# First layer of a graph network kernel: the messages and a copy of the run flags in two free PSUM banks

## The chip, the cores and the metric

The kernel runs on one core of a Trainium2 chip. The metric is the device time of one execution in microseconds, the median of several runs. The core has five engines that run their own instruction streams and meet on semaphores: TensorE (PE: matmuls, and PEld: its weight loads), VectorE (DVE), ScalarE (ACT), GpSimd (POOL) and SyncE (SP, which here issues plain DMAs). POOL also issues the indirect DMAs, those that take their addresses from a table of indices in SBUF. PSUM has eight banks; a bank holds 512 fp32 elements in each of 128 partitions.

## The reference, cut to what matters

Four graph layers on 12500 nodes with 16 features and 400000 edges, each preceded by a layer norm and a ReLU. The change touches the first layer only, which applies the weighted adjacency four times:

```python
def step(y, _):
    msg = weights[:, None] * y[col]
    y_new = jax.ops.segment_sum(msg, row, num_segments=N_NODES)
    return (y_new, None)
y, _ = jax.lax.scan(step, x, None, length=LAYER_NUMBER)   # LAYER_NUMBER = 4
```

Here `col` is the edge's `dst`, by which the edges come sorted, and `row` its `src`.

## The kernel before, in words

The function `powers` computes the first layer in four rounds, one for each application. Before it the edges have been put into an order by their target: 132 turns (`G_TURNS`), each of 25 columns of 128 edges (`TURN`). Two turns make a pair (`PAIR`), 66 pairs a round, 264 pairs in all. Within a partition the edges of a turn lie so that those that read the same node follow each other as a run. So a node's row has to be written only where a run starts; a scan along the columns carries it through the run. `goes_on` holds the run flags (0 where a run starts, 1 where it goes on; a 16-bit type).

In each round the engines do this:

- POOL scatters the node rows from SBUF (`by_b`) to the places in HBM (`filled`) at which runs start, with one indirect DMA for 128 rows (line 1651), addresses from the table `at_start` in SBUF. The rows are cut into blocks of 8 such DMAs (2 in the last block of each of the 7 groups of 13 blocks), 91 blocks and 686 DMAs a round. After every 6 DMAs it rests (ten tiny memsets and a wait). It also gathers the first row of each turn (`first`, line 1654), 132 DMAs a round. When all DMAs of a block have landed, it raises `blocks_ready` (line 1631), and it does so behind the issues of the block after it.
- SP waits, turn by turn, for `blocks_ready` to reach the block that the turn needs, and for `expanded`, by which VectorE tells that one of four buffers is free (lines 1606 and 1607), and loads the turn's 25 columns into `given`.
- VectorE takes a pair at a time: it waits for the pair's two loads, puts the first rows in (line 1676), runs 16 scans, one for each feature, over 50 columns (line 1681, result `along`), builds the one-hot of the target's low digit (`a_hot`, 1684) and a copy of its high digit (`b_val`, 1686), and multiplies by the edge weights (`message`, 1688). Then come ten slots of five columns: `spread` is the product of `a_hot` and `message` (640 elements, line 1527), and two or three of the five one-hot rows `b_hot` are VectorE's too (line 1530).
- ScalarE makes the other `b_hot` rows (lines 1538 and 1544).
- TensorE multiplies `spread` and `b_hot` into the sums in PSUM (line 1549): five matmuls a slot, each of which is two records in the trace, 100 a pair. `spread` and `b_hot` are rings of five slots: VectorE waits for `taken` before it writes a slot, TensorE for `ready` and `warmed` before it reads one.

The order on each engine is the order of the code. `Gathering` holds four PSUM banks for the sums and two for the transposes at the end of a round. The tiles that the change touches stand so:

```python
        along = s.sb("along", [P, PAIR * TURN, D])
        message = s.sb("message", [P, PAIR * TURN, D])
```

Of the kernel before, what the change touches and what calls it, by code (L numbers as in the profile page):

```python
# [14 lines left out]
P = 128  # L15
N_NODES = 12500
N_EDGES = 400000
D = 16
# [7 lines left out]
TURN = TILES * SLOTS  # L26
# [555 lines left out]
PIECE = 512  # L582
# [647 lines left out]
PAIR = 2  # L1230
# [292 lines left out]
def spread_slot(dve, message, a_hot, spread, b_val, b_hot, c, ready, own):  # L1523


    n = message.shape[1]
    dve.tensor_tensor(spread, a_hot.unsqueeze(3).to_broadcast([P, n, 8, D]),  # L1527
                      message.unsqueeze(2).to_broadcast([P, n, 8, D]), ALU.mult)
    for j in range(own):
        ins = dve.tensor_scalar(b_hot[:, j, :], c.wide[:], b_val[:, j:j + 1], None, ALU.is_equal)  # L1530
    ins.then_inc(ready, 1)
# [23 lines left out]
def powers(nc, c, G, weight, goes_on, first_node, starts, filled, node_rows, H, Y, rounds):  # L1555
# [6 lines left out]
    with Scope(nc, "powers") as s:  # L1562
# [3 lines left out]
        given = s.sb("given", [P, G_RING, TURN, D])  # L1566
        first = s.sb("first", [P, G_TURNS, D])
        along = s.sb("along", [P, PAIR * TURN, D])
        message = s.sb("message", [P, PAIR * TURN, D])
        a_hot = s.sb("a_hot", [P, PAIR * TURN, 8])  # L1570
        b_val = s.sb("b_val", [P, PAIR * TURN])
        spread = s.sb("spread", [P, SLOTS, TILES, 8, D])
# [89 lines left out]
        @block.vector  # L1662
        def _(dve):
            dve.memset(g.zeros[:], 0.0).then_inc(g.blank, 1)
            dve.sem_inc(expanded, G_RING)
            with dve.Fori(0, rounds) as r:
                with dve.Fori(0, G_TURNS // G_RING) as it:
                    for h in range(G_RING // PAIR):
                        pair = it * (G_RING // PAIR) + h
                        n = r * (G_TURNS // PAIR) + pair  # L1670
                        ks = slice(h * PAIR, (h + 1) * PAIR)
                        cols = bass.ds(pair * (PAIR * TURN), PAIR * TURN)
                        for given_sem in given_in[ks]:
                            dve.wait_ge(given_sem, r * (G_TURNS // G_RING * 16) + it * 16 + 16)
                        dve.wait_ge(firsts_ready, (n + 1) * PAIR)
                        dve.tensor_scalar(given[:, ks, 0, :], first[:, bass.ds(pair * PAIR, PAIR), :],
                                          1.0, None, ALU.mult).then_inc(begun, 1)
                        dve.wait_ge(begun, n + 1)
                        rows = given[:, ks].rearrange("p k c f -> p (k c) f")
                        for f in range(D):  # L1680
                            ins = dve.tensor_tensor_scan(along[:, :, f], goes_on[:, cols], rows[:, :, f], 0.0,
                                                         ALU.mult, ALU.add)
                        ins.then_inc(expanded, PAIR)
                        dve.tensor_tensor(a_hot[:], G.a[:, cols].unsqueeze(2).to_broadcast([P, PAIR * TURN, 8]),
                                          c.free[:, 0:8].unsqueeze(1).to_broadcast([P, PAIR * TURN, 8]), ALU.is_equal)
                        dve.tensor_scalar(b_val[:], G.minus_b[:, cols], -1.0, None, ALU.mult)
                        dve.wait_ge(expanded, (n + 1) * PAIR + G_RING)
                        dve.tensor_tensor(message[:], along[:], weight[:, cols].unsqueeze(2)
                                          .to_broadcast([P, PAIR * TURN, D]), ALU.mult).then_inc(mid, 1)
                        dve.wait_ge(mid, n + 1)  # L1690
                        for j in range(PAIR * SLOTS):
                            dve.wait_ge(taken, n * (PAIR * SLOTS) + j + 1)
                            at = slice(j * TILES, (j + 1) * TILES)
                            spread_slot(dve, message[:, at], a_hot[:, at], spread[:, j % SLOTS], b_val[:, at],
                                        b_hot[:, j % SLOTS], c, ready, OWN[j % 2])
                        dve.wait_ge(ready, (n + 1) * (PAIR * SLOTS))
# [1170 lines left out]
def gnn_kernel(nc, x, src, dst, edge_attr_2, edge_attr_8, edge_type_8, edge_weight, L1_gnn_weight, L2_gnn_W1,  # L2867
# [5 lines left out]
    with ExitStack() as ctx:  # L2873
# [15 lines left out]
        with Scope(nc, "g") as gs:  # L2889
# [35 lines left out]
            with Scope(nc, "l0") as s:  # L2925
                weight = s.sb("weight", [P, G_COLS])
                load_places(nc, c, grouped, G, weight, goes_on, first_node, pair_rows, through_rows)
                layernorm(nc, "ln0", X, H)
                powers(nc, c, G, weight, goes_on, first_node, starts, filled, node_rows, H, Y, 4)
# [57 lines left out]
```

## Time and profile before

| | us |
|---|---|
| median of three runs | 17761.85 |
| lowest and highest | 17757.97, 17768.52 |
| the profiled execution | 17890.86 |
| its span, first to last instruction | 17889.0 |
| busy: PE, PEld | 14307.1, 13410.2 |
| busy: DVE, ACT, POOL | 14538.7, 11808.6, 10642.2 |
| the first layer (`powers`) in the span | about 2760 to 8760 |

The busy times are totals over stages that differ. For the first layer the profile is read by stretches: each round has a stretch in which POOL issues DMAs and a short one at its end in which POOL has nothing left to do. The granted clock in the tables (PEclk) is the mean over a stretch, 1.00 being TensorE's full speed.

### The profile page before, as it was taken

What the parts mean: (1) busy time and instruction counts of PE and PEld (TensorE: products, weight loads), DVE (VectorE), ACT (ScalarE), POOL (GpSimd) and SP (SyncE); (2) the same over time, 40 slices, a digit from 0 to 9 for tenths busy, and PEclk for the clock granted to TensorE, in tenths of its full rate; (3) what the DMA queues carried; (4) which work ended last, traced back from release to release, by engine and by line L of the source; (5) the groups of instructions that cost most, each with busy time, mean ns of one, the idle gap of its engine ahead of it and who ended that gap; (6) DMA issues with size and microseconds to landing.
All of it is one profiled execution on the core that took longest, in us unless ns stands there. A gap on an engine that the chain in (4) does not pass through costs nothing. (4 is left out here: it accounts for less than half of the span.)

```text
span 17889.0 us, 349943 instructions
## 1 busy us (share of the span) xinstructions
PE 14307.1 (80%) x83251; PEld 13410.2 (75%) x83252; DVE 14538.7 (81%) x36176; ACT 11808.6 (66%) x23445; POOL 10642.2 (59%) x29948
## 2 busy tenths in 40 slices
PE   0148846998998899898699997899829999499997
PEld 0048846888888888788688886788718888399996
DVE  4745556887887888788699997999929999599997
ACT  2000015877777777777577776999919999477775
POOL 0458846775775777577477774666662445477710
PEclk9555558999999999999899998999969999699998
DMA  7611131000000001000111112222212222111111
GB/s 236 127 24 39 39 82 25 24 23 22 23 24 22 23 24 25 21 24 23 31 32 31 31 29 46 79 74 80 76 26 68 74 75 73 36 31 31 30 27 16
DMA packets 1268448, 826.81 MB, mean 46 GB/s; under 512 B 873459, under 2 KB 1213399, under 8 KB 1260759
## 3 DMA queue, kind: packets, MB, share of 16 engines
q1 hardware_dynamic: 880918, 671.78, 13.3%
q0 software_dynamic: 269056, 117.80, 3.4%
q10 hardware_dynamic: 118080, 33.61, 1.1%
q14 instruction: 345, 2.82, 0.1%
q8 instruction: 49, 0.80, 0.0%
HBM read 587.33 MB, written 235.06 MB: 46 GB/s over the span
## 5 line engine op out<-in xcount | busy, mean ns | idle before, releaser
L1549 PE MATMUL powers_sums<-powers_b_hot,powers_spread 128*128 128x224 f32 x26400 | 5286.2, 362 | 680.9 <-DVE powers_b_hot L1530 475.5
L1549 PEld LDWEIGHTS powers_sums<-powers_b_hot,powers_spread 128*128 128x128 f32 x26400 | 5101.1, 195 | 868.2 <-issue 833.5
L1651 POOL DMA_INDIRECT filled<-powers_by_b,powers_at_start x2688 | 3366.2, 1252 | 1744.2 <-issue 834.8
L1544 ACT ACTIVATE powers_b_hot<-powers_away,ones 128x672 f32<-128x672 f32 x2640 | 1980.0, 752 | 1259.6 <-PE powers_sums L1549 905.5
L1538 ACT ACTIVATE powers_away<-wide,powers_minus_b 128x224 f32<-128x224 f32 x6600 | 2719.3, 472 | 117.5 <-ACT powers_minus_b L1719 37.6
L1527 DVE TENSOR_TENSOR powers_spread<-powers_a_hot,powers_message 128x640 f32<-128x640 f32 x2640 | 2155.0, 816 | 487.4 <-PE powers_sums L1549 306.8
L2356 PE MATMUL relate_got<-relate_hot,relate_table 112*128 112x512 f32 x10560 | 2119.0, 344 | 172.3 <-ACT relate_hot L2317 79.9
L2356 PEld LDWEIGHTS relate_got<-relate_hot,relate_table 112*128 112x128 f32 x10560 | 1628.0, 194 | 437.5 <-issue 117.1
L2372 PE MATMUL relate_mixed<-relate_mix,relate_picked 128*128 128x128 f32 x13200 | 1814.2, 286 | 159.7 <-DVE relate_picked L2421 79.9
L1530 DVE TENSOR_SCALAR powers_b_hot<-wide,powers_b_val 128x224 f32<-128x224 f32 x6600 | 1922.1, 339 | 0.0
L2317 ACT ACTIVATE relate_hot<-relate_away,ones 112x1280 fp32r<-112x1280 bf16 x1320 | 1781.8, 1350 | 206.7 <-DMA conv_given<-filled 114.0
L2372 PEld LDWEIGHTS relate_mixed<-relate_mix,relate_picked 128*128 128x128 f32 x13200 | 1613.2, 195 | 282.2 <-issue 218.4
L2649 POOL DMA_INDIRECT relate_ends<-rec,g_ends x1176 | 1223.0, 1040 | 721.3 <-issue 453.9
L1111 PE MATMUL place_made<-place_spread,place_row_hot 125*105 125x80 f32 x6400 | 1183.5, 385 | 347.1 <-DVE place_spread L1161 287.9
L1111 PEld LDWEIGHTS place_made<-place_spread,place_row_hot 125*105 125x105 f32 x6400 | 1145.9, 297 | 384.9 <-issue 192.5
L1096 ACT COPY place_rows<-place_made 105x320 f32<-105x320 f32 x200 | 85.2, 426 | 2006.9 <-PE place_made L1111 1825.4
L1549 PE MATMUL conv_sums<-conv_b_hot,conv_spread 128*128 128x224 f32 x6600 | 1364.4, 354 | 23.7 <-issue 23.7
L1549 PE MATMUL message_sums<-message_b_hot,message_spread 128*128 128x224 f32 x6600 | 1357.1, 353 | 0.0
L1080 POOL DMA_INDIRECT grouped<-place_rows,place_at x800 | 1084.7, 1356 | 263.6 <-issue 218.5
L1896 POOL DMA_INDIRECT filled<-conv_by_b,conv_at_start x728 | 879.8, 1209 | 603.3 <-POOL conv_still L1495 239.4
L1549 PEld LDWEIGHTS conv_sums<-conv_b_hot,conv_spread 128*128 128x128 f32 x6600 | 1199.9, 190 | 39.2 <-issue 38.9
L1549 PEld LDWEIGHTS message_sums<-message_b_hot,message_spread 128*128 128x128 f32 x6600 | 1198.9, 190 | 0.5
(478 smaller groups left out, 25665.5 us busy)
## 6 DMA issues: line engine op xcount, KB each, us to landing
relate_codes<-pair_rows SPq DMA_DIRECT2D x264, 800.0 KB
powers_given<-filled SPq DMA_DIRECT2D x528, 200.0 KB
rec<-relate_running SPq DMA_DIRECT2D x132, 400.0 KB
filled<-powers_by_b,powers_at_start POOLq DMA_INDIRECT x2688
grouped<-order_blanks POOLq DMA_DIRECT2D x20, 1320.0 KB
filled<-order_blanks SPq DMA_DIRECT2D x20, 1320.0 KB
held_recs<-grouped SPq DMA_DIRECT2D x132, 200.0 KB
conv_given<-filled SPq DMA_DIRECT2D x132, 200.0 KB
```

Of the source, the lines that this page charges most:

```text
L1080: pool.indirect_dma_start(flat, bass.IndirectOffsetOnAxis(at[0:PACKED, k, q:q + 1], 0), rows[0:PACKED, k, q, :], None).then_inc(sent[q], 16)
L1111: mm = pe.matmul(made[0:PACKED, k, q * ROW * WORDS:(q + 1) * ROW * WORDS], row_hot[0:SPAN, k % 2, q * CELL + t, :], spread[0:SPAN, k % 2, ...
L1527: dve.tensor_tensor(spread, a_hot.unsqueeze(3).to_broadcast([P, n, 8, D]), message.unsqueeze(2).to_broadcast([P, n, 8, D]), ALU.mult)
L1530: ins = dve.tensor_scalar(b_hot[:, j, :], c.wide[:], b_val[:, j:j + 1], None, ALU.is_equal)
L1538: ins = act.activation(away[:, j, :], c.wide[:], ACT.Abs, bias=minus_b[:, j:j + 1], scale=1.0)
L1544: act.activation(b_hot, away, ACT.Relu, bias=c.ones[:, 0:1], scale=-1.0).then_inc(warmed, 1)
L1549: mm = pe.matmul(gathering.sums[:, bass.ds(group * STRIDE, WINDOW)], spread[:, j].rearrange("p a d -> p (a d)"), b_hot[:, j, :], start=Fal ...
L1651: pool.indirect_dma_start(filled, bass.IndirectOffsetOnAxis(to, 0), rows, None).then_inc(spread_out[block % 2], 16)
L2317: act.activation(hot[:, n % HOTS], away[:, n % 2], ACT.Relu, bias=c.ones[0:HALF, 0:1], scale=-1.0).then_inc(hotted, 1)
L2356: mm = pe.matmul(got[:, n % 2, at:to], table[:, n // SLOTS % 2, part, half, :], flat[:, at:to], start=half == part == 0, stop=half == part ...
L2372: mm = pe.matmul(mixed[:, n % 2, k * P:(k + 1) * P], picked[:, n % 2, k, :], mix[:].rearrange("i o r -> i (o r)"), start=True, stop=True)
L2649: pool.indirect_dma_start(to[:, h, :], None, sums, bass.IndirectOffsetOnAxis(G.ends[:, h, g:g + 1], 0)).then_inc(ends_in, 16)
```

## The change: what it does

A new tile `held` of two PSUM banks takes the place of `message` in SBUF: 800 of its 1024 fp32 elements hold the pair's messages, and the next 50 hold `onward`, a copy of the pair's run flags. VectorE makes this copy at the head of each pair, and the 16 scans read `onward` in place of `goes_on`. The multiply by the weights writes to PSUM, and the ten `spread` multiplies of a pair read one operand from SBUF (`a_hot`) and one from PSUM (the message). `begun` now counts two instructions of a pair. No work is left out, and no other function changes.

```diff
@@ powers: tiles
-        message = s.sb("message", [P, PAIR * TURN, D])
+        held = s.ps("held", [P, 2 * PIECE])
+        message = held[:, 0:PAIR * TURN * D].rearrange("p (c d) -> p c d", d=D)
+        onward = held[:, PAIR * TURN * D:PAIR * TURN * (D + 1)]
@@ powers: VectorE, each pair
                         cols = bass.ds(pair * (PAIR * TURN), PAIR * TURN)
+                        dve.tensor_copy(onward, goes_on[:, cols]).then_inc(begun, 1)
                         for given_sem in given_in[ks]:
                             dve.wait_ge(given_sem, r * (G_TURNS // G_RING * 16) + it * 16 + 16)
                         dve.wait_ge(firsts_ready, (n + 1) * PAIR)
                         dve.tensor_scalar(given[:, ks, 0, :], first[:, bass.ds(pair * PAIR, PAIR), :],
                                           1.0, None, ALU.mult).then_inc(begun, 1)
-                        dve.wait_ge(begun, n + 1)
+                        dve.wait_ge(begun, (n + 1) * 2)
                         rows = given[:, ks].rearrange("p k c f -> p (k c) f")
                         for f in range(D):
-                            ins = dve.tensor_tensor_scan(along[:, :, f], goes_on[:, cols], rows[:, :, f], 0.0,
+                            ins = dve.tensor_tensor_scan(along[:, :, f], onward, rows[:, :, f], 0.0,
                                                          ALU.mult, ALU.add)
                         ins.then_inc(expanded, PAIR)
...
-                        dve.tensor_tensor(message[:], along[:], weight[:, cols].unsqueeze(2)
+                        dve.tensor_tensor(message, along[:], weight[:, cols].unsqueeze(2)
                                           .to_broadcast([P, PAIR * TURN, D]), ALU.mult).then_inc(mid, 1)
```

On VectorE this is the program of one pair before the change, from its head to the first slot; names that begin with `powers_` are tiles of this function, `g_goes_on` is `goes_on`, and the rows ISA are waits.

```order
L1675 ISA
L1676 ISA
L1676 TENSOR_SCALAR powers_given<-powers_first 128x2x16
L1681 ISA
L1681 SCALAR_TENSOR_TENSOR powers_along<-g_goes_on,powers_given 128x50 x16
L1684 REGISTER_ALU
L1684 TENSOR_TENSOR powers_a_hot<-g_g_a,free 128x400
L1686 REGISTER_ALU
L1686 TENSOR_SCALAR powers_b_val<-g_g_minus_b 128x50
L1687 REGISTER_ALU
L1688 ISA
L1688 TENSOR_TENSOR powers_message<-powers_along,l_weight 128x800
```

After the change the same place on VectorE reads as follows.

```order
L1675 COPY powers_held<-g_goes_on 128x50
L1677 ISA
L1678 ISA
L1679 ISA
L1679 TENSOR_SCALAR powers_given<-powers_first 128x2x16
L1684 SCALAR_TENSOR_TENSOR powers_along<-powers_held,powers_given 128x50 x16
L1687 REGISTER_ALU
L1687 TENSOR_TENSOR powers_a_hot<-g_g_a,free 128x400
L1689 REGISTER_ALU
L1689 TENSOR_SCALAR powers_b_val<-g_g_minus_b 128x50
...
L1691 ISA
L1691 TENSOR_TENSOR powers_held<-powers_along,l_weight 128x800
```

One instruction is new, the copy, and it stands ahead of the waits for the pair's data; nothing else has moved. The first operand of the 16 scans and the output of the last multiply are now in `held`.

The slots that follow, on VectorE before the change:

```order
L1527 TENSOR_TENSOR powers_spread<-powers_a_hot,powers_message 128x640
L1530 TENSOR_SCALAR powers_b_hot<-wide,powers_b_val 128x224 x2
L1692 REGISTER_ALU
L1527 TENSOR_TENSOR powers_spread<-powers_a_hot,powers_message 128x640
L1530 TENSOR_SCALAR powers_b_hot<-wide,powers_b_val 128x224 x3
```

And after it:

```order
L1527 TENSOR_TENSOR powers_spread<-powers_a_hot,powers_held 128x640
L1530 TENSOR_SCALAR powers_b_hot<-wide,powers_b_val 128x224 x2
L1695 REGISTER_ALU
L1527 TENSOR_TENSOR powers_spread<-powers_a_hot,powers_held 128x640
L1530 TENSOR_SCALAR powers_b_hot<-wide,powers_b_val 128x224 x3
```

The order is the same; only the second operand of the `spread` multiply has changed its place.

## Rows read from the trace of the kernel before

**Rows 1.** Windows: four stretches with POOL issuing, and one without (7138 to 7247).

```profile
2813.00:4136.00 1323.00, 1201.28 (x5962) 1153.44 (x5963) 1101.30 (x3295) 1025.68 (x2135) 1018.37 (x1886) 0.95 0.10 24
...
4316.00:5631.00 1315.00, 1201.53 (x5945) 1150.79 (x5946) 1100.70 (x3292) 1024.01 (x2132) 1014.18 (x1884) 0.96 0.10 24
...
5810.00:7138.00 1328.00, 1200.30 (x5968) 1158.41 (x5969) 1101.65 (x3300) 1028.97 (x2143) 1028.71 (x1882) 0.95 0.10 23
7138.00:7247.00 109.00, 109.00 (x577) 108.58 (x576) 103.97 (x321) 99.88 (x209) 9.55 (x16) 1.00 0.07 19
7314.00:8625.00 1311.00, 1192.13 (x5950) 1151.08 (x5951) 1096.77 (x3292) 1022.70 (x2134) 1010.42 (x1878) 0.95 0.10 24
```

**Rows 2.** VectorE's pair heads: a whole round, then POOL silent (min/median/max, first and last).

```profile
L1676 DVE TENSOR_SCALAR powers_given<-powers_first x66: 181/182/385, 2812.7 to 4236.4; 128x32 f32 x66
...
L1676 DVE TENSOR_SCALAR powers_given<-powers_first x5: 181/182/183, 4160.4 to 4236.4; 128x32 f32 x5
```

**Rows 3.** Waits of VectorE in rounds one and four; of SP's queue, all rounds.

```profile
DVE powers_given L1676 <- DMA powers_given<-filled: 46.5, 9, 7.7
...
DVE powers_given L1676 <- DMA powers_given<-filled: 56.8, 9, 10.7
...
SPq L1606 <- POOLq L1631: 3951.1, 307, 25.3
...
SPq L1607 <- DVE powers_along L1681: 247.7, 25, 17.2
```

**Rows 4.** Groups on POOL in the first layer; one DMA's duration (min/median/max).

```profile
L1651 POOL DMA_INDIRECT filled<-powers_by_b,powers_at_start x2688 | 3366.2, 1252 | 1744.2 <-issue 834.8 <-DMA node_rows<-powers_by_b 387.3 <-DMA powers_by_b<-node_rows 284.3
L1654 POOL DMA_INDIRECT powers_first<-node_rows,g_first_node x528 | 608.2, 1152 | 160.8 <-issue 160.8
...
L1651 POOL DMA_INDIRECT filled<-powers_by_b,powers_at_start x2688: 956/962/4187, 2772.0 to 8635.1; - x192
```

**Rows 5.** Timeline, head of one pair: start, us, engine, line.

```profile
5019.03 2.60 DVE L1681 TENSOR_TENSOR_SCAN powers_along<-g_goes_on,powers_given 128x50 f32<-128x50 f32 x16 [0.25 <-DVE powers_given L1676]
...
5020.76 3.20 POOL L1651 DMA_INDIRECT filled<-powers_by_b,powers_at_start  x1 [0.30 <-issue]
5021.53 0.56 DVE L1684 TENSOR_TENSOR powers_a_hot<-g_g_a,free 128x400 f32<-128x400 f32 x1
5022.00 0.19 DVE L1686 TENSOR_SCALAR powers_b_val<-g_g_minus_b 128x50 f32 x1
5022.10 0.99 DVE L1688 TENSOR_TENSOR powers_message<-powers_along,l_weight 128x800 f32<-128x800 f32 x1
```

**Rows 6.** Timeline in the third layer, where the multiplies read PSUM.

```profile
12215.52 0.73 DVE L2456 TENSOR_TENSOR_SCAN relate_running<-g_goes_on,relate_message 128x50 f32<-128x50 f32 x4
...
12215.74 1.32 POOL L2649 DMA_INDIRECT Y<-rec,g_ends  x1 [0.30 <-issue]
...
12216.16 0.81 DVE L2435 TENSOR_TENSOR relate_product<-relate_mixed,relate_share 128x640 f32<-128x640 f32 x1
...
12216.88 0.88 DVE L2421 SCALAR_TENSOR_TENSOR relate_picked<-relate_codes,relate_lanes,relate_got 128x640 f32<-128x640 uint8 x1
```

**Rows 7.** By tile and line: VectorE with an operand in PSUM, then without.

```profile
L856 DVE TENSOR_TENSOR_SCAN ranks_so_far_g<-ranks_one,ranks_so_far_g,ranks_sums x120: 286/295/321, 470.9 to 954.1; 128x50 f32<-128x50 f32 x120
...
L856 DVE TENSOR_TENSOR_SCAN ranks_so_far_g<-ranks_one,ranks_sums x8: 232/233/253, 445.3 to 446.4; 128x50 f32<-128x50 f32 x8
...
L2435 DVE TENSOR_TENSOR relate_product<-relate_mixed,relate_share x1320: 785/802/857, 11030.7 to 15471.8; 128x640 f32<-128x640 f32 x189
...
L1681 DVE TENSOR_TENSOR_SCAN powers_along<-g_goes_on,powers_given x4224: 224/241/341, 2813.4 to 8726.4; 128x50 f32<-128x50 f32 x192
...
L1527 DVE TENSOR_TENSOR powers_spread<-powers_a_hot,powers_message x2640: 804/815/885, 2817.6 to 8740.3; 128x640 f32<-128x640 f32 x189
```

**Rows 8.** Waits of TensorE and VectorE on each other, all rounds.

```profile
PE powers_sums L1549 <- DVE powers_b_hot L1530: 475.5, 111, 63.8
...
DVE powers_spread L1527 <- PE powers_sums L1549: 306.8, 265, 7.0
```

## The prediction

> **What bounds the kernel now.** I read the stretches first. While POOL issues its DMAs, TensorE makes 23825 records in the four stretches' 5277 us, 221.5 ns each; when POOL has nothing left to issue, 577 in 109 us, 189 ns each, at a granted clock of 1.00 [rows 1]. The same shows in VectorE's pair heads: 65 steps from 2812.7 to 4236.4 us, 21.9 us a pair, against four steps from 4160.4 to 4236.4, 19.0 us a pair, once POOL is silent [rows 2]. A pair costs TensorE 100 x 189 ns = 18.9 us, and VectorE's own pair is no shorter than that either: the two are even. So what slows the first layer comes with POOL. The most there is to win is 5277 - 23825 x 0.189 = 774 us over four rounds.
>
> What is it? Three things. First, the data are late: after the first pair of a round VectorE still waits for its loads, 46.5 us in round one and 56.8 us in round four, 215 us in all four [rows 3]. Second, the clock: its mean is 0.95 to 0.96 in the POOL stretches, and 5% of 5277 us is some 250 us [rows 1]; that is the lower level (1.2 GHz) for about a tenth of the time, and since it is 1.00 in the quiet stretch, where TensorE is never without work, I put its falls down to the standstills. Third, the rest, 774 - 215 - 250 = about 310 us, hand-offs between two even engines: TensorE waited 475.5 us for VectorE (four round starts of about 60 us included), VectorE 306.8 us for TensorE [rows 8].
>
> Who makes the data late? SP's queue waited 3951.1 us for POOL's block count and only 247.7 us for a free buffer [rows 3]: the loads go out as POOL releases them. POOL starts round one at 2772.0 us and is done at about 4136 us, 1364 us or 20.7 us a pair, more than the 19.0 us that a pair needs [rows 1, 2, 4]. POOL sets the pace.
>
> And why is POOL slow? Its indirect DMAs take 962 ns in the median but 4187 ns at most; the 2688 scatters and 528 gathers are busy for 3366.2 + 608.2 = 3974.4 us, where 962 ns each would be 3094 us. The 880 us on top are 3.3 us a pair, 220 us a round [rows 4]. The timeline of a pair shows where they arise: the DMA that POOL begins at 5020.76, inside the scans, ends at 5023.96, that is 0.87 us after the weight multiply's end at 5023.09. It was held through scans, `a_hot`, `b_val` and message, and ran when these were over [rows 5]. All but `b_val` read two operands from SBUF. The third layer shows the other case: a DMA begun at 12215.74 inside a run of four scans that ends at 12216.25 takes 1.32 us, so it ends 0.81 us after the run, although VectorE goes straight on with a multiply and then the pick at line 2421 [rows 6]. These two read `mixed` and `got`, which are PSUM tiles, and POOL isn't held by them.
>
> **The change, part by part.**
>
> The scans read PSUM and `given`. The part of the pair's head that can hold POOL shrinks from 5019.03 to 5023.09 (4.06 us) to 5021.53 to 5023.09 (1.56 us): `a_hot` has two SBUF operands still, and so has the weight multiply, which only writes to PSUM [rows 5]. If all of the 880 us arose at the head, 880 x 2.50 / 4.06 = 542 us would go; if most came from elsewhere the ten `spread` multiplies are the only other long pair of SBUF operands, and the change frees these too, so the bound on that side is all 880 us. I take 640 us, nearer to the head's share since the rows show the long holds there: 160 us a round. POOL's round falls from 1364 to about 1204 us, 18.2 us a pair: below 19.0, so POOL no longer sets the pace.
>
> What the scans cost themselves: a scan of 50 with its second operand in PSUM took 233 ns in the median, the scans here with both in SBUF 241 ns. Another form with one in PSUM, which also takes its start value from a tile, took 295 ns. The multiply with a PSUM operand took 802 ns, `spread` 815 ns [rows 7]. The form here has a constant start like the first, so I take nothing for either, and 295 - 241 = 54 ns for the high end; -8 and -13 ns would be -0.26 us a pair, some -70 us over the layer if VectorE alone were the bound. The Trainium skill speaks against the change here ("VectorE: DVE Perf Modes", the section on the TRN2 errata): its table gives a fixed 58 cycles for VectorE from SBUF and 120 from PSUM. By that, an estimate, 26 instructions a pair would each be 65 ns longer, 1.7 us a pair. By it the sum would be up to 264 x 1.7 = 446 us worse. The two rows with a PSUM operand and no start tile show none of it.
>
> The write of the message to PSUM has no row: the trace has no VectorE instruction that writes PSUM. Nearest is the present write, 0.99 us [rows 5]. I bound it by nothing below and by a second such instruction above (+0.99 us a pair, 261 us), and take nothing, since reads show no difference.
>
> The copy is 50 elements, the size of `b_val`, after which the next instruction starts 0.10 us later [rows 5]. It is hidden where the pair's data are late, and on VectorE's path where they aren't, which is to be the rule after the change: 264 x 0.10 = 26 us. At the most it costs 0.19 us, `b_val`'s whole duration: 50 us. No new wait hangs on another engine; `begun` waits for VectorE's own copy, which is issued ahead of `given`'s write.
>
> What then comes back: of the 215 us of late data I count 180, because TensorE would have stood briefly at some of those heads anyway (VectorE pauses for its scans). Of the 250 us of clock I count 100: fewer standstills, so fewer falls, but in round one the clock isn't full all along between late loads either. The hand-offs stay. Next late is VectorE itself, whose 19.1 us a pair stand against TensorE's 18.9. The sum: -180 - 100 + 26 = -254 us. On the profiled execution (span 17889.0, time 17890.86) that makes 17637; it is 129 us above the median, 17761.85, from which the same difference gives **17510 us**, 1.4% less.
>
> **The rivals.**
>
> 1. POOL is held by something else than the second SBUF operand, say the scans' writes. For it: the third layer's row has one operand in PSUM and a shorter run, so it shows release under multiplies, not under scans. Against it: the write to SBUF is there in those multiplies too. Then only the copy counts: +26 us, 17790.
> 2. POOL is relieved, but the layer goes at VectorE's pace anyway: the lost 310 us of hand-offs grow by what the late data leave, and the clock falls as often. Then the data waits alone shrink, in part: -60 us, 17700. Against it: stretches without POOL run at 19.0 us and full clock with the same VectorE program [rows 1, 2].
> 3. PSUM operands are slower on VectorE than their two rows say. Its pair is 19.1 + x; with the clock's losses left (250 / 264 = 0.95 us) it reaches the present 21.9 us at x = 1.85 us, or 71 ns for each of 26 instructions. At 54 ns each, the high end above, x is 1.4 and the time changes by 264 x (19.1 + 0.95 + 1.4 - 21.9) = -119 us, 17640. The Trainium skill's errata table, quoted above, would put x at 1.7, just short of the point where nothing is left of the gain.
> 4. Slower: the same with 100 ns each, x = 2.6 us, most of it in the write of the message and in the wait for it, so that every `spread` of the pair starts later while TensorE runs dry at each head. 264 x 0.75 = +198 us, 17960. Against it: the 233 ns scans.
> 5. A larger gain: with an even supply the clock stays up and the hand-offs shrink as in the quiet stretches. -215 - 200 - 30 + 26 = about -420 us, 17340. It is the forecast's own upper half rather than a different mechanism.
>
> **How the numbers follow.** The forecast with rival 5 has 0.71 (0.05 of it beyond rival 5's figure), rival 1 0.09, rival 2 0.08, rival 3 0.06, rival 4 0.06. The range takes the forecast, rival 5's figure as its low end and rival 2's as its high end, 17340 to 17710; outside are rivals 1 and 4 and the tail of 5, 0.20 together. About 0.2% (36 us) is what a measurement of this kernel can tell from no change. Most of rival 1 falls within it, and of rivals 2 and 3 the part that brings less than reckoned, 0.05: same 0.13; slower 0.08, of rival 4 and of rival 1 with a dear copy (0.02); faster 0.79.
>
> **What would show it.** In the profile after: POOL's DMAs of line 1651 near 1.0 us in the mean (now 1252 ns) and none of 3 us that begins inside the scans; POOL's stretch about 160 us shorter a round; VectorE's waits for its loads nearly gone after each round's first pair; the clock above 0.96 in the POOL stretches; scans at about 233 ns and `spread` at 802 to 815; SP waiting for buffers where it waited for blocks. The prediction is wrong if POOL's mean stays (rival 1), if scans or `spread` are longer (3, 4), or if POOL is quick and the pairs stay above 21 us (2).

## The result and the profile after

The changed kernel takes 17131.72 us (median of 4 runs, 17109.55 to 17138.83), the kernel before 17760.31 us: a ratio of 0.9642, with a 95% interval of 0.9628 to 0.9655. It is 629 us faster. I had said 17510, with 17340 as the low end: the direction and the cause (POOL is freed) were right, the gain was far too small. The profiled executions have spans of 17889.0 and 17127.7 us, 761 us apart. The stretch of the first layer's matmuls explains 646 us of it (its rows stand below); the rest lies ahead of and behind the layer, where the program is the same, and is not seen in the medians: the profiled execution of before was itself 129 us above its median.

The first layer's stretches after the change, by windows (us from the start; busy time and count of PE, PEld, DVE, ACT, POOL; granted clock; DMA share and GB/s): four with POOL issuing and one without.

```profile
2755.00:3886.00 1131.00, 1112.40 (x5821) 1099.67 (x5822) 1080.59 (x3281) 1004.97 (x2091) 825.30 (x1897) 1.00 0.11 28
3886.00:4030.00 144.00, 144.00 (x763) 143.77 (x762) 134.36 (x415) 125.56 (x261) 0.99 (x2) 1.00 0.05 14
4086.00:5214.00 1128.00, 1107.40 (x5786) 1092.62 (x5787) 1077.74 (x3266) 998.87 (x2078) 825.04 (x1898) 1.00 0.11 27
5421.00:6552.00 1131.00, 1106.66 (x5772) 1090.78 (x5773) 1077.10 (x3249) 996.69 (x2072) 828.16 (x1898) 0.99 0.11 27
6764.00:7894.00 1130.00, 1110.63 (x5803) 1096.43 (x5804) 1079.93 (x3274) 1002.50 (x2086) 825.22 (x1897) 0.99 0.11 28
```

Beside [rows 1]: TensorE now makes 23182 records in 4520 us, 195 ns each where it was 221.5, and the clock has gone from 0.95 to 1.00 or 0.99. The two kinds of stretch are nearly alike (763 in 144 us is 189 ns each).

VectorE's pair heads after the change, round one and then the part of it with POOL silent:

```profile
L1679 DVE TENSOR_SCALAR powers_given<-powers_first x66: 181/182/398, 2754.6 to 4007.7; 128x32 f32 x66
L1679 DVE TENSOR_SCALAR powers_given<-powers_first x5: 181/181/182, 3932.3 to 4007.7; 128x32 f32 x5
```

Beside [rows 2]: 65 steps of 19.3 us, where they were 21.9. With POOL silent a pair is 18.9 us, as it was 19.0 before, so VectorE's own program has become neither shorter nor longer by anything that shows.

Groups of the first layer on POOL after the change (busy us, mean ns, then idle time before them):

```profile
L1653 POOL DMA_INDIRECT filled<-powers_by_b,powers_at_start x2664 | 2627.1, 986 | 1558.6 <-issue 721.7 <-DMA node_rows<-powers_by_b 492.3 <-POOL powers_still L1495 344.6
L1656 POOL DMA_INDIRECT powers_first<-node_rows,g_first_node x519 | 520.7, 1003 | 158.1 <-issue 157.8 <-DMA filled<-powers_by_b,powers_at_start 0.3
```

Beside [rows 4]: a scatter takes 986 ns in the mean, not 1252. The timeline of one pair's head shows why.

```profile
3508.96 0.21 DVE L1675 CAST powers_held<-g_goes_on 128x50 f32 x1 [0.16 <-DVE powers_b_hot L1530]
3509.30 0.18 DVE L1679 TENSOR_SCALAR powers_given<-powers_first 128x32 f32 x1
...
3509.52 2.54 DVE L1684 TENSOR_TENSOR_SCAN powers_along<-powers_held,powers_given 128x50 f32<-128x50 f32 x16
3509.78 0.96 POOL L1653 DMA_INDIRECT filled<-powers_by_b,powers_at_start  x1 [0.31 <-issue]
3511.05 0.96 POOL L1653 DMA_INDIRECT filled<-powers_by_b,powers_at_start  x1 [0.30 <-issue]
...
3511.98 0.55 DVE L1687 TENSOR_TENSOR powers_a_hot<-g_g_a,free 128x400 f32<-128x400 f32 x1
3512.32 1.04 POOL L1653 DMA_INDIRECT filled<-powers_by_b,powers_at_start  x1 [0.30 <-issue]
```

Beside [rows 5]: two DMAs run inside the scans at their full speed, where the one of before took 3.20 us.

The waits after the change, of VectorE, of TensorE and of SP's queue in the first layer (us in total, times, longest):

```profile
DVE powers_given L1679 <- DMA powers_given<-filled: 245.1, 9, 61.3
...
DVE powers_spread L1527 <- PE powers_sums L1549: 4.5, 11, 0.6
...
PE powers_sums L1549 <- DVE powers_b_hot L1530: 266.2, 91, 63.2
...
SPq L1608 <- POOLq L1633: 2579.7, 273, 29.1
SPq L1609 <- DVE powers_along L1684: 1710.5, 157, 17.0
```

Beside [rows 3, 8]: of the 245.1 us in which VectorE waited for its loads, nearly all is the four round starts of about 60 us. VectorE no longer waits for TensorE (306.8 us before), and TensorE waits 266.2 us for VectorE where it was 475.5; this too is mostly the round starts. SP's queue waits for a free buffer seven times as long as before, and for POOL less. VectorE's own instructions with an operand in `held`, by tile (min/median/max ns, first and last start):

```profile
L1684 DVE TENSOR_TENSOR_SCAN powers_along<-powers_held,powers_given x4224: 225/238/268, 2754.9 to 8021.5; 128x50 f32<-128x50 f32 x192
L1527 DVE TENSOR_TENSOR powers_spread<-powers_a_hot,powers_held x2640: 800/808/828, 2759.2 to 8035.5; 128x640 f32<-128x640 f32 x189
L1675 DVE CAST powers_held<-g_goes_on x264: 212/214/215, 2695.7 to 8018.6; 128x50 f32 x132
L1691 DVE TENSOR_TENSOR powers_held<-powers_along,l_weight x264: 981/995/1248, 2757.9 to 8022.2; 128x800 f32<-128x800 f32 x132
```

The scans are 3 ns and the spreads 7 ns shorter than in [rows 7]. The write of the message, for which no row stood ahead, has a median of 995 ns against 0.99 us; its mean is 1023 ns while it was 986, and 994 with POOL silent.

### The profile page after: what moved, and what is told of

The parts are those of the page before. It is cut to its first block and busy times, and to the rows that moved or that the text cites. A ratio compares the mean times of both kernels' runs of the same rounds, so it can differ in the third digit from the quotient of the medians.

```text
span 17127.7 us, 350207 instructions
## 1 busy us (share of the span) xinstructions
PE 14056.0 (82%) x83251; PEld 13296.5 (78%) x83252; DVE 14576.9 (85%) x36440; ACT 11806.2 (69%) x23445; POOL 9814.4 (57%) x29948
## 5 line engine op out<-in xcount | busy, mean ns | idle before, releaser
L1549 PE MATMUL powers_sums<-powers_b_hot,powers_spread 128*128 128x224 f32 x26400 | 5047.4, 354 | 274.0 <-DVE powers_b_hot L1530 266.2
L1549 PEld LDWEIGHTS powers_sums<-powers_b_hot,powers_spread 128*128 128x128 f32 x26400 | 4987.5, 191 | 336.1 <-issue 332.1
L1653 POOL DMA_INDIRECT filled<-powers_by_b,powers_at_start x2688 | 2650.2, 986 | 1848.6 <-issue 727.8
L1527 DVE TENSOR_TENSOR powers_spread<-powers_a_hot,powers_held 128x640 f32<-128x640 f32 x2640 | 2137.4, 810 | 41.9 <-PE powers_sums L1549 4.5
```

What stands on the lines that cost most here:

```text
L1549: mm = pe.matmul(gathering.sums[:, bass.ds(group * STRIDE, WINDOW)], spread[:, j].rearrange("p a d -> p (a d)"), b_hot[:, j, :], start=Fal ...
L1653: pool.indirect_dma_start(filled, bass.IndirectOffsetOnAxis(to, 0), rows, None).then_inc(spread_out[block % 2], 16)
```

## The experiments

Two theories stood after the result. **Pace:** POOL's pace sets the layer's time, and late loads, falls of the clock and hand-off waits are only the forms in which this wait shows; VectorE's instructions with two SBUF operands had slowed POOL. **VectorE:** the gain comes from VectorE's own pair (PSUM operands, or the copy at its head), which takes TensorE's standstills away.

### Message only, flags only, copy only

```diff
# e1_message_only, against the change: the scans read the flags from SBUF, no copy
-                        dve.tensor_copy(onward, goes_on[:, cols]).then_inc(begun, 1)
...
-                            ins = dve.tensor_tensor_scan(along[:, :, f], onward, rows[:, :, f], 0.0,
+                            ins = dve.tensor_tensor_scan(along[:, :, f], goes_on[:, cols], rows[:, :, f], 0.0,
# e2_flags_only, against the change
+        message = s.sb("message", [P, PAIR * TURN, D])[:]
...
-        message = held[:, 0:PAIR * TURN * D].rearrange("p (c d) -> p c d", d=D)
-        onward = held[:, PAIR * TURN * D:PAIR * TURN * (D + 1)]
+        onward = held[:, 0:PAIR * TURN]
# e3_copy_in_sbuf, against the change: no tile in PSUM is left
...
+        message = s.sb("message", [P, PAIR * TURN, D])[:]
+        onward = s.sb("onward", [P, PAIR * TURN])[:]
```

> Only the message is in PSUM; the scans read the run flags from SBUF as before, without the copy. Theory (supply): POOL was held by VectorE's instructions with two SBUF operands, and POOL's pace set everything else. The spreads no longer hold it, the scans do, so POOL's round falls from 1369 us (first to last issue, before) only to about 1310 us, 19.9 us a pair, still slower than VectorE's 19.2: the time is 100 to 300 us below before, around 17550, with some late loads and a clock between 0.95 and 1.00. Rival (VectorE): the gain comes from VectorE's own pair or from reading the message in PSUM, which takes TensorE's standstills away; then this kernel has most of the 629 us, 17200.

> Only the copy of the run flags is in PSUM; the message is in SBUF as before. Supply theory: the scans don't hold POOL, the ten spreads do; POOL's round about 1240 us, 18.8 us a pair, just under VectorE's 19.2, so nearly the whole gain: 17150 to 17250. Rival (VectorE, by the message): little of the gain, above 17500.

> The copy of the run flags is made at the head of each pair, but into SBUF, and the message is in SBUF: the change's instructions without PSUM. Supply theory: POOL stays at 1369 us a round and the time at that of before, 17760 to 17800. Rival (order): the copy at the head takes the wait for VectorE's own last one-hot rows and the branch off the pair's path; then a part of the gain shows here, 17500 or less.

Measured: the message alone 17548.98 us (ratio 0.9875, 0.9859 to 0.9892), the flags alone 17143.19 (0.9645, 0.9629 to 0.9661), the copy in SBUF 17774.08 (1.0001, 0.9992 to 1.0011), with 17771.79 for the kernel before. All three came out as the pace theory had them, the flags alone 7 us below its range. The copy and its place in the program are worth nothing while POOL sets the pace; with POOL silent the copy-only kernel's pairs are 18.9 us too. Reading the flags from PSUM is worth nearly all; the message alone is worth a third, and on top of the flags nothing that shows (17143 against 17132). The groups on POOL of the message-only, the flags-only and the copy-only kernel, one line each:

```profile
L1652 POOL DMA_INDIRECT filled<-powers_by_b,powers_at_start x2688 | 3158.9, 1175 | 1728.4 <-issue 727.0 <-DMA node_rows<-powers_by_b 364.3 <-POOL powers_still L1495 347.2
```

```profile
L1653 POOL DMA_INDIRECT filled<-powers_by_b,powers_at_start x2688 | 2794.4, 1040 | 1741.5 <-issue 727.7 <-DMA node_rows<-powers_by_b 377.9 <-POOL powers_still L1495 347.2
```

```profile
L1652 POOL DMA_INDIRECT filled<-powers_by_b,powers_at_start x2688 | 3335.5, 1241 | 1718.2 <-issue 724.6 <-DMA node_rows<-powers_by_b 358.3 <-POOL powers_still L1495 347.2
```

Means of 1175, 1040 and 1241 ns, with 1252 before and 986 after: the same copy frees POOL when it lies in PSUM and not when it lies in SBUF. The copy-only kernel shows something more, in VectorE's waits:

```profile
DVE powers_given L1678 <- DMA powers_given<-filled: 822.5, 104, 61.7
...
DVE powers_spread L1527 <- PE powers_sums L1549: 90.5, 217, 0.6
```

Its time is that of before, but its late loads are 822.5 us where [rows 3] add up to 459 with the round starts, and its waits for TensorE 90.5 us where [rows 8] have 306.8. The parts move and the sum stays. The copy isn't what moves them: the kernel before with short rests (below), which has no copy, has 826.1 and 93.2 us. So the profiled execution of before splits the time in its own way, and the two others agree with each other.

### A slowed POOL

```diff
# e4_slow_pool, against the change
-        still, rested = s.sb("still", [P, RESTS]), s.sem("rested")      # RESTS = 10
+        still, rested = s.sb("still", [P, 56]), s.sem("rested")
# e9_gathers_twice, against the change: each first-row gather a second time, into a tile that nobody reads
-                        pool.wait_ge(first_in[half], r * (16 * first_counts(half)) + 16 * upto)
+                        pool.wait_ge(first_in[half], r * (32 * first_counts(half)) + 32 * upto)
...
+                        pool.indirect_dma_start(spare[:, turn, :], None, node_rows,
+                                                bass.IndirectOffsetOnAxis(first_node[:, turn:turn + 1], 0)
+                                                ).then_inc(first_in[block % 2], 16)
```

> The changed kernel with POOL slowed in this layer alone: 56 tiny memsets instead of 10 in each of its 113 rests a round, about 1.7 us more each, so that its round is about 1365 us as before, while VectorE's program is that of the change. Supply theory: late loads, falls of the clock and hand-off waits all come back with it, the time rises to 17650 to 17800. Rival (each loss has a cause of its own; only the late loads hang on POOL's pace): 200 us of late loads come back, the clock in the POOL stretches stays at 0.98 or above, 17350.

Measured: 17658.69 us (0.9941, 0.9925 to 0.9958), in the range of the pace theory. But the run doesn't prove it. VectorE waited 279.4 us for its loads, hardly more than the round starts, so the late loads had not come back; the clock in round one's POOL stretch was 0.98, as the rival had it; and VectorE's one-hot rows had grown from 343 to 409 ns in the mean. The timeline shows the long memsets holding them:

```profile
4510.20 2.20 DVE L1530 TENSOR_SCALAR powers_b_hot<-wide,powers_b_val 128x224 f32<-128x224 f32 x2
4510.23 1.80 POOL L1495 MEMSET powers_still<- 128x1 f32 x56
```

Two one-hot rows that take 0.57 us otherwise take 2.20 us. At 25 rows a pair the growth of the mean is 1.6 us a pair, so VectorE's own pair was about 21 us. This kernel slowed POOL and VectorE both, and a second way to slow POOL was needed, one without more memsets.

> The changed kernel, in which POOL gathers each turn's first rows twice, the second time into a spare tile that nobody reads: 132 more indirect DMAs a round of 1.27 us, so its round goes from 1171 to about 1339 us, with no more memsets. Theory (law of the pace, from the runs so far): a round of the layer takes the longer of POOL's round + 110 us and VectorE's 1321 us; here 1449 us, so 4 x 128 = 512 us more than the change, 17640; late loads or a lower clock come with it, and the one-hot rows keep their 343 ns. Rival (the slow-POOL kernel was slow since its memsets held VectorE's one-hot rows): without more memsets nothing changes, 17130 to 17200.

Measured: 17636.19 us (0.9933, 0.9917 to 0.995), against 17640 expected. Its groups on VectorE and its waits:

```profile
L1530 DVE TENSOR_SCALAR powers_b_hot<-wide,powers_b_val 128x224 f32<-128x224 f32 x6600 | 1956.9, 344 | 0.0
...
DVE powers_given L1683 <- DMA powers_given<-filled: 706.0, 89, 69.5
...
PE powers_sums L1549 <- DVE powers_b_hot L1530: 659.1, 103, 73.1
```

The one-hot rows are at 344 ns and VectorE's program is that of the change, yet late loads (706.0 us), TensorE's waits (659.1 us) and the lower clock all come back; in round one, by windows, it is 0.96 (0.95 to 0.96 in all four stretches with POOL issuing):

```profile
2818.00:4117.00 1299.00, 1196.11 (x6087) 1177.76 (x6088) 1135.20 (x3430) 1051.31 (x2189) 917.77 (x1948) 0.96 0.11 25
```

This is what tells cause from effect: on the compute engines nothing but POOL's work was changed. The 132 more gathers a round move little (the DMA share is 0.11 with them and without).

### Shorter rests

```diff
# e5_before_short_rests, against the kernel before; e8_after_short_rests and c2, against the change
-        still, rested = s.sb("still", [P, RESTS]), s.sem("rested")
+        still, rested = s.sb("still", [P, 1]), s.sem("rested")
```

> The kernel before, with one memset instead of ten in each rest of the first layer; nothing in PSUM. POOL's 113 rests a round are some 0.33 us shorter each, 37 us a round: from 1369 to about 1332 us. Law of the pace: 4 x 37 = 150 us less, about 17610. Rival (the hold of POOL by two SBUF operands matters in a way of its own, not by POOL's pace): within 40 us of before.

Measured: 17704.96 us with 17752.4 before (0.9974, 0.9963 to 0.9986), some 50 us instead of 150. Neither the 150 us of the theory nor the rival's 40 at most. POOL's round did not shrink by 37 us: from its first to its last scatter, round one took 1359 us where it was 1364, and the mean of the four rounds fell from 1365.5 to 1354.7, which makes 43 us for the layer. The rests are shorter, but POOL's DMAs became longer, scatters 1269 ns against 1252 and gathers 1241 against 1152 (the copy-only kernel, with its ten memsets, has 1241 and 1267):

```profile
L1651 POOL DMA_INDIRECT filled<-powers_by_b,powers_at_start x2688 | 3410.8, 1269 | 1716.7 <-issue 714.2 <-DMA node_rows<-powers_by_b 362.5 <-POOL powers_still L1495 353.3
L1654 POOL DMA_INDIRECT powers_first<-node_rows,g_first_node x528 | 655.5, 1241 | 160.9 <-issue 160.9
```

So what POOL won in its rests it lost in part in its DMAs. The time went with POOL's actual rounds (43 us by them, 47 measured), as the pace theory has it, but my figure for the round was wrong; why the DMAs grew was not tested.

> The changed kernel with one memset instead of ten in each rest of the first layer. POOL is not the bound, so its 37 us a round give nothing by themselves. But if the memsets hold VectorE's one-hot rows, as they did in the slow-POOL kernel (409 ns against 343), the rows fall from 343 to about 332 ns, 25 x 11 ns = 0.27 us a pair, 70 us in all: 17060. Rival (memsets this few hold nothing that counts): 17130 within 20 us.

Measured: 17101.26 us (0.9628, 0.9612 to 0.9644). That is in neither range: the one-hot rows came to 340 ns, not 332, and the gain was 30 us, less than half of what I expected. To see whether it is there at all, both ran once more side by side, five times each:

> The changed kernel once more, on the same chip as the next one: 17110 to 17140.

> The changed kernel with one memset instead of ten in each rest of the first layer, beside the change itself. If the 30 us of the first comparison are real, it is 17090 to 17110, about 0.2% below the change; if they were the chip's scatter, the two are equal within 15 us.

The change took 17135.69 us (17125.07 to 17145.96), the one with short rests 17111.2 (17093.89 to 17120.87); the ranges don't overlap, as they didn't the first time, so I take about 24 us or 0.14% as real. What they come from isn't shown: 25 rows a pair, each 3 ns shorter, would be 20 us over the layer, but POOL's round is shorter too. It is the fastest kernel of this study.

### All runs in one table

POOL's round is from the first to the last scatter of round one; the layer's share is a quarter of the stretch from the first to the last matmul record. The two rows of the kernel before, then of the change, then of the kernel with doubled gathers show where these are read (by tile and by line):

```profile
L1651 POOL DMA_INDIRECT filled<-powers_by_b,powers_at_start x672: 956/962/4103, 2772.0 to 4135.9; - x168
L1549 PE MATMUL powers_sums<-powers_b_hot,powers_spread x26400: 349/352/737, 2819.4 to 8749.3; 128*128 128x224 f32 x199
```

```profile
L1653 POOL DMA_INDIRECT filled<-powers_by_b,powers_at_start x672: 952/958/1647, 2713.6 to 3882.8; - x168
L1549 PE MATMUL powers_sums<-powers_b_hot,powers_spread x26400: 352/353/738, 2761.1 to 8044.6; 128*128 128x224 f32 x199
```

```profile
L1654 POOL DMA_INDIRECT filled<-powers_by_b,powers_at_start x672: 952/958/1728, 2719.4 to 4057.3; - x168
L1549 PE MATMUL powers_sums<-powers_b_hot,powers_spread x26400: 352/353/739, 2776.5 to 8573.7; 128*128 128x224 f32 x199
```

| kernel | POOL's round | layer / 4 | difference | median us |
|---|---|---|---|---|
| before | 1364 | 1482 | 118 | 17760 |
| copy in SBUF | 1377 | 1481 | 104 | 17774 |
| before, short rests | 1359 | 1465 | 106 | 17705 |
| gathers twice | 1338 | 1449 | 111 | 17636 |
| slow POOL (56 memsets) | 1327 | 1449 | 122 | 17659 |
| message only | 1312 | 1421 | 109 | 17549 |
| flags only | 1202 | 1321 | 119 | 17143 |
| the change | 1169 | 1321 | 152 | 17132 |
| change, short rests | 1139 | 1315 | 176 | 17101 |

Down to POOL's 1202 us the layer follows POOL's round at a distance of 104 to 119 us: the start of a round, and the pairs that are left when POOL is done. (The row of the slow POOL doesn't count here, since VectorE was slowed as much.) Below 1202 POOL's round falls by another 63 us and the layer by 6 only. There VectorE's pair is the bound, with TensorE's close behind: VectorE waits neither for loads, but at the round starts, nor for TensorE. 264 pairs of 19.3 us and three starts of 60 us between rounds are 5275 us, and the stretch is 5284.

Why 19.3 us and not the 18.9 with POOL silent? VectorE's one-hot rows show most of it, in POOL's stretch of round one and then in the one behind it:

```profile
L1530 DVE TENSOR_SCALAR powers_b_hot<-wide,powers_b_val 128x224 f32<-128x224 f32 x1460 | 430.9, 343 | 0.0
L1530 DVE TENSOR_SCALAR powers_b_hot<-wide,powers_b_val 128x224 f32<-128x224 f32 x191 | 53.6, 331 | 0.0
```

12 ns for each of 25 rows are 0.3 us a pair. They are there with one memset a rest too (342 and 327 ns), so the memsets are not all of it; what else of POOL's work lengthens them was not tested.

## Why the prediction was wrong

**What bounds the kernel.** Right: POOL set the pace, and the DMAs held behind two-SBUF-operand instructions were the reason. The three single changes show that the place of the operand decides, the doubled gathers that POOL's pace does.

**POOL's relief.** I took 640 us of a bound of 880. The groups show scatters and gathers busy 3974.4 us before and, scaled from 3183 records in the view to 3216, 3180 us after: about 790 us. POOL's round one fell by 195 us, not 160. This term was mis-sized, but harmless: at 1204 us, my figure, the layer is already where POOL stops being the bound, as the flags-only kernel shows with 1202.

**VectorE's own costs.** I counted nothing for reads and writes in PSUM and 26 us for the copy. Scans at 238 ns, spreads at 808 and the write at 995 bear out the first. The copy was dearer than the 0.10 us that I took: it lasts 214 ns, and in the timeline above the next instruction starts 0.34 us after it. Its cost still doesn't show, since the pairs with POOL silent are no longer than before, 18.9 us; the copy-only kernel (1.0001) can't tell, because POOL sets its pace. The difference of 62 cycles between SBUF and PSUM in the errata table of the Trainium skill's "VectorE: DVE Perf Modes" shows in none of these rows.

**What then comes back: the step that failed.** I split the 774 us that POOL's stretches lose into 215 us of late loads, 250 of clock and about 310 of hand-offs, and let 180, 100 and nothing come back. Of the 774 us some 635 came back: 4520 us less 23182 records of 0.189 us leaves 139. The late loads went nearly whole (the 245.1 us that are left are round starts of about 60 us, but for some 7), so did the clock's 250, and so, by what remains, did about 190 of the 310 for hand-offs, which I had put at nothing without a reason. I had treated three readings of one wait as three losses with causes of their own. They aren't: an engine that is fed too slowly shows it as a late load here, as a fallen clock there and as a full ring behind the slow matmuls elsewhere. The copy-only kernel splits the same time otherwise, and with the gathers doubled all three come back together.

I had the numbers that would have done better: POOL's 20.7 us a pair against VectorE's 19.0 [rows 2] (the 19.1 that I wrote stands in no row). By the longer of the two, the layer after the change is 264 x 19.0 + 3 x 60 = 5196 us where the profile of before has 5930, 734 us less at the most; the profiles have 646, as a pair took 19.3 us beside POOL, and the median fell by 629. I wrote "POOL no longer sets the pace" and then did not draw the round from the next pace.

**The rivals.** The first and the third fell (POOL was freed, PSUM operands cost nothing that shows), as did the fourth, the slower one. The second, that VectorE's pace keeps the gain small, had the right next bound and the wrong price: that bound lay 161 us a round below. The fifth had the direction, but stopped at 420 us because it also summed shares.

## What to carry to other kernels

When a producer sets the pace, forecast the stage as the longest of the engines' own paces, before and after, plus the fixed start and end, and expect the next engine's pace beside a busy neighbour to be a little longer than alone; don't price its symptoms one by one, since late data, a fallen clock and waits between the consumers can be one loss in three columns. Look at which VectorE instructions read two operands from SBUF while GpSimd issues indirect DMAs, runs of short ones above all: here one copy of 50 elements into PSUM, 0.21 us a pair, took the hold from 16 of them and brought nearly the whole gain. And when a probe slows an engine, check that it slows that one only.

## What the runs showed of the hardware that I had not expected

POOL's tiny memsets hold VectorE too, and not only where it reads two SBUF operands: the one-hot rows read one tile and a per-partition scalar, and two of them took 2.20 us instead of 0.57 under 56 memsets; with 56, 10 and 1 memsets a rest their mean was 409, 343 and 340 ns, and with POOL silent 331. And the granted clock in the layer's POOL stretches went from 0.95 to 1.00 with no change in TensorE's program: here an even supply of work was enough, and with the gathers doubled it fell again, to 0.95 to 0.96.
